# Graph kernel on one core: seven gathered slots in the third pass in place of six, counts scaled by ScalarE there

## The reference

```
for l in range(3):
    neigh = segment_sum(h[src], dst) / clip(deg, 1)
    h = h @ Ws_self[l] + neigh @ Ws_neigh[l] + bs[l]      (relu but for the last)
x = layernorm(x + h)
hs, hv = x[:, :128] @ w_in2f_s, einsum(x[:, 128:], w_in2f_v)     (32 + 3*32 numbers for each node)
W = (ssp(edge_attr_20 @ W1 + b1) @ W2 + b2) * edge_weight
edge = products of hs[idx_j], hv[idx_j], edge_attr_4 and W
agg = segment_sum(edge, idx_i)                            (idx_i = src, idx_j = dst)
x = layernorm(x + two small matrix products of agg)
```

## Time and profile before

| | us |
|---|---|
| median of 3 runs | 1892.74 (1888.39 to 1895.12) |
| profiled execution, its own time | 1891.2 |
| its span | 1889.4 |
| third pass, tile 50 to the last message row's store | about 1142 to 1457 |
| message phase | about 1459 to 1889 |
| busy PE, DVE, POOL, ACT | 1827.0, 1180.4, 1180.8, 627.3 |

### The profile page before, as it was taken

One profiled execution on the slowest core, in us unless ns is written; L12 is line 12 of the kernel. 1 busy time (PEld: TensorE's weight loads), 2 busy tenths in 40 slices (PEclk: granted clock), 3 DMA queues, 4 the chain that ended last, 5 costly groups with the idle time before them and its releaser, 6 DMA issues. The chain is left out here.

```text
span 1889.4 us, 23661 instructions
## 1 busy us (share of the span) xinstructions
PE 1827.0 (97%) x8259; PEld 1160.8 (61%) x8259; DVE 1180.4 (62%) x1811; ACT 627.3 (33%) x1432; POOL 1180.8 (62%) x1082
## 2 busy tenths in 40 slices
PE   7999999999999999999999998999998999999997
PEld 3454455555555555555555555666666888888886
DVE  5766678677644344343343344555553899999997
ACT  1566632233000000000000000111103888888885
POOL 4400000165588888888888883788886777777773
PEclk9999999999999999999999999999998999999999
DMA  5365566443454435444444434555564344434442
GB/s 156 108 218 182 202 217 185 124 115 104 129 143 138 123 107 147 134 134 124 117 130 122 114 98 156 179 190 195 195 196 133 89 116 116 113 108 107 108 117 56
DMA packets 235894, 261.88 MB, mean 139 GB/s; under 512 B 130678, under 2 KB 173280, under 8 KB 235773
## 3 DMA queue, kind: packets, MB, share of 16 engines
q1 hardware_dynamic: 200956, 204.29, 35.6%
q0 software_dynamic: 34032, 55.66, 11.0%
q10 hardware_dynamic: 784, 0.39, 0.1%
HBM read 172.52 MB, written 87.69 MB: 138 GB/s over the span
## 5 line engine op out<-in xcount | busy, mean ns | idle before, releaser
L1208 PE MATMUL low<-table,abuf 125*125 125x512 f16 x3750 | 835.2, 380 | 0.0
L1208 PEld LDWEIGHTS low<-table,abuf 125*125 125x125 bf16 x3750 | 506.4, 137 | 303.0 <-issue 27.9
L905 POOL DMA_INDIRECT by_src<-scat_row,sort x416 | 502.7, 1208 | 126.1 <-issue 118.8
L1037 PE MATMUL mid<-wbuf,h_t 128*125 128x512 f32 x1200 | 557.2, 601 | 14.0 <-DVE st_out L1733 10.9
L910 POOL DMA_INDIRECT table<-msg_table,wbuf x294 | 316.8, 1078 | 97.8 <-issue 97.5
L1037 PEld LDWEIGHTS mid<-wbuf,h_t 128*125 128x125 f32 x1200 | 214.9, 189 | 222.1 <-issue 198.2
L1743 DVE SCALAR_TENSOR_TENSOR y<-low,inv_deg,st_in 125x512 f32<-125x512 f32 x75 | 56.2, 749 | 446.6 <-PE low L1208 328.1
L1687 DVE TENSOR_TENSOR abuf<-abuf,row_scale 125x3125 bf16<-125x3125 bf16 (+4 forms) x87 | 256.9, 2956 | 1.2 <-DMA abuf<-adj 1.2
L937 POOL DMA_INDIRECT sort<-msg_table,sort x156 | 202.0, 1295 | 63.9 <-issue 47.2
L888 POOL TENSOR_TENSOR sort<-sort 128x416 f32<-128x416 f32 x26 | 31.8, 1224 | 329.9 <-DVE sort L1805 329.9
L1242 PE MATMUL low<-table,wbuf 128*125 128x256 f32 x900 | 209.9, 383 | 21.0 <-ACT table L1466 20.9
(11 more groups left out here) (244 smaller groups left out, 1616.6 us busy)
## 6 DMA issues: line engine op xcount, KB each, us to landing
abuf<-adj SPq DMA_DIRECT2D x75, 781.2 KB, 5.0
adj<-table SPq DMA_DIRECT2D x25, 781.2 KB, 4.5
states<-st_out SPq DMA_DIRECT2D x75, 256.0 KB, 2.3
st_in<-states SPq DMA_DIRECT2D x75, 256.0 KB, 4.9
flips<-y_flip SPq DMA_DIRECT2D x48, 256.0 KB, 4.3
h_t<-flips SPq DMA_DIRECT2D x192, 64.0 KB
early_rows<-sort POOLq DMA_DIRECT2D x30, 320.0 KB, 2.7
table<-early_rows SPq DMA_DIRECT2D x24, 384.0 KB, 6.5
```

The costliest lines, as they stand in the source:

```text
L905: pool.indirect_dma_start(out=by_src, out_offset=bass.IndirectOffsetOnAxis(ap=place_i[:, k * PIECE + j:k * PIECE + j + 1], axis=0), in_=sc ...
L1037: last = pe.matmul(to[0:TN, :], h_t[i % 2][:, k, 0:TN], weights[l % 2][:, a, k, :], start=k == 0, stop=k == KC - 1)
L1208: last = pe.matmul(p_agg[k % 2][0:TN, :], a_tile[k % 3][:, a, :], table[ps % 2][0:TN, a, h, :], start=a == 0 and h == 0, stop=a == TILES - ...
```

## The change

- Seven slots of every source tile (`EARLY = 7`) are gathered in the third pass, 35 steps in place of 30. The gathers, the store and the load of tile 0's second group go. In the message phase GpSimd gathers slots 7 to 17 of all 25 tiles: 275 gathers, 11 for each tile, tile 0 among them. The load of one tile's early slots is 448 KB where it was 384, and its buffer is waited for until group 1 (not 0) of two tiles back is through.
- For k = 52 to 74 the counts are scaled by ScalarE: 25 activations of 125x125 (L1403 of the changed file), 16 ahead of the eviction of the transposes and 9 behind it. TensorE waits for the two parts at `a = 0` and `a = 16`. VectorE's L1687 is left out for these tiles.

```diff
+EARLY = 7
+STEPS = EARLY * CHUNKS
@@
-            return 16 * (t // 2 + 1)
-        return 16 * GS * (t // 2 + (0 if g == 1 and t % 2 == 0 else 1))
+        return 16 * (t // 2 + 1) * {0: 1, 1: 2 * GS - EARLY}.get(g, GS)
@@
+        return {0: (0, 22, 23, 24, 25), 1: (0, 23, 25)}.get(k % TILES, (0, 16, 25) if k > 2 * TILES else (0, 25))
+
+    def by_act(k):
+
+        return 2 * TILES + 1 < k < AGGS
@@ load_early (SP)
-                    sp.wait_ge(s_gd, 3 * NG * (t - 2) + 3)
+                    sp.wait_ge(s_gd, 3 * (NG * (t - 2) + 1) + 3)
@@
-            sp.wait_ge(s_est[SECOND % 3], loads_of(SECOND, 3))
-            sp.dma_start(msg_slots[0][:, GS:2 * GS, :], second_rows.rearrange("p (j k) -> p j k", j=GS)).then_inc(s_second, 16)
@@ GpSimd, windows of the early slots
-            pool.dma_start(e_swin, edges_of[:, 0, GS:2 * GS, :]).then_inc(s_ewin[0], 16)
...
-                               edges_of[:, lo:hi, 0:GS, :].rearrange("p t j k -> p t (j k)")).then_inc(s_ewin[n], 16)
+                               edges_of[:, lo:hi, 0:EARLY, :].rearrange("p t j k -> p t (j k)")).then_inc(s_ewin[n], 16)
@@ GpSimd, early steps
-            steps_of = [(j, c) for j in range(GS) for c in range(CHUNKS)]
+            steps_of = [(j, c) for j in range(EARLY) for c in range(CHUNKS)]
...
-            gather_second()
             store_early(*steps_of[-1])
-            store_second()
@@ GpSimd, message phase
-                for g in range(1 if t else 2, NG):
+                for g in range(1, NG):
                     if t >= 2:
                         pool.wait_ge(s_gd, 3 * (NG * (t - 2) + g) + 3)
-                    for j in range(g * GS, (g + 1) * GS):
+                    for j in range(max(g * GS, EARLY), (g + 1) * GS):
@@ ScalarE
+            def scale(k, part):
+                parts = parts_of(k)
+                if part == 0:
+                    act.wait_ge(s_a[k % 3], loads_of(k, 3))
...
+                for a in range(parts[part], parts[part + 1]):
+                    last = act.activation(a_tile[k % 3][:, a, :], a_tile[k % 3][:, a, :], ACT.Copy, scale=row_scale[k // TILES % 2][0:TN, a:a + 1])
+                last.then_inc(s_as, 1)
@@
                     root(i - AGGS + 1)
+                    if by_act(k + 1):
+                        scale(k + 1, 0)
                     transposed(i, ACT.Copy)
+                    if by_act(k + 1):
+                        scale(k + 1, 1)
                     message_rows(i)
@@ VectorE
-                if k + 1 < AGGS:
+                if k + 1 < AGGS and not by_act(k + 1):
                     scale(k + 1, 0)
...
-                if t == 0 and g == 1:
-                    dve.wait_ge(s_second, 16)
-                else:
-                    dve.wait_ge(s_g[g][t % 2], slots_gathered(t, g))
+                dve.wait_ge(s_g[g][t % 2], slots_gathered(t, g))
```

More of the change, by code:

```diff
@@ L171, in gnn_kernel @@
     early = Region(sort_sb[:, :], 7 * CH * 4)
-    e_rows = [early.take(P, [GS, G]) for _ in range(3)]
-    e_idx = early.take(P, [TILES, GS], I32)
-    e_second = early.take(P, [GS], I32)
-    e_f = early.take(P, [GS, TILES])
-    e_fs = early.take(P, [GS])
-    e_max = early.take(P, [GS + 1])
-    e_most = early.take(1, [GS + 1])
-    e_below = early.take(1, [GS + 1, TILES])
-    e_need = early.take(1, [GS + 1], I32)
+    e_rows = [early.take(P, [FEW, G]) for _ in range(3)]
+    e_idx = early.take(P, [TILES, EARLY], I32)
+    e_f = early.take(P, [EARLY, TILES])
+    e_max = early.take(P, [EARLY])
+    e_most = early.take(1, [EARLY])
+    e_below = early.take(1, [EARLY, TILES])
+    e_need = early.take(1, [EARLY], I32)
     x_rows = Region(sort_sb[:, :], 7 * CH * 4).take(P, [SLOTS, G])
@@ L277, in gnn_kernel @@
     ereg = Region(wbuf[:, :, :].rearrange("p a k -> p (a k)"), 2 * 2 * KC * D * 4)
-    e_win = ereg.take(P, [TILES, GS, PAY])
-    e_swin = ereg.take(P, [GS, PAY])
+    e_win = ereg.take(P, [TILES, EARLY, PAY])
     treg = Region(tbuf[0][:, :], T_SIZE)
@@ L467, in early_gathered @@
     def early_gathered(s):
-        return 16 * sum(GS if n == SECOND else FEW for n in range(s % 3, s + 1, 3))
+        return 16 * FEW * (s // 3 + 1)
     def slots_gathered(t, g):
-        if g == 0:
-            return 16 * (t // 2 + 1)
-        return 16 * GS * (t // 2 + (0 if g == 1 and t % 2 == 0 else 1))
+        return 16 * (t // 2 + 1) * {0: 1, 1: 2 * GS - EARLY}.get(g, GS)
     def node_rows(t):
@@ L775, in _ @@
                 if k == AGGS - 4:
-                    sp.wait_ge(s_eidx, len(PARTS_OF) + 1)
+                    sp.wait_ge(s_eidx, len(PARTS_OF))
                 if k >= AGGS - 4 and k < AGGS - 1:
@@ L807, in load_early @@
                 if t >= 2:
-                    sp.wait_ge(s_gd, 3 * NG * (t - 2) + 3)
+                    sp.wait_ge(s_gd, 3 * (NG * (t - 2) + 1) + 3)
                 c, i = t // FEW, t % FEW
                 if t == 1 or i == 0:
-                    for j in range(GS):
+                    for j in range(EARLY):
                         s = early_step(j, c)
                         sp.wait_ge(s_est[s % 3], loads_of(s, 3))
-                sp.dma_start(msg_slots[t % 2][:, 0:GS, :], early_rows[:, c, :, i * G:(i + 1) * G].rearrange("j p k -> p j k")).then_inc(s_g[0][t % 2], 16)
+                sp.dma_start(msg_slots[t % 2][:, 0:EARLY, :], early_rows[:, c, :, i * G:(i + 1) * G].rearrange("j p k -> p j k")).then_inc(s_g[0][t % 2], 16)
             extras(sp, extra_round)
-            sp.wait_ge(s_est[SECOND % 3], loads_of(SECOND, 3))
-            sp.dma_start(msg_slots[0][:, GS:2 * GS, :], second_rows.rearrange("p (j k) -> p j k", j=GS)).then_inc(s_second, 16)
             for t in range(TILES):
@@ L915, in extra_round @@
                 wait_alone(pool, s_xl, q * 32)
-                for s in range(SECOND - 2, SECOND + 1):
+                for s in range(STEPS - 3, STEPS):
                     pool.wait_ge(s_est[s % 3], loads_of(s, 3))
@@ L1193, in _ @@
                         pe.wait_ge(s_emax, 1)
-                        for n in range(GS + 1):
+                        for n in range(EARLY):
                             top = pe.transpose(p_b[n // 4][0:1, n % 4 * P:(n % 4 + 1) * P], e_max[:, n:n + 1], ident[:, :])
@@ L1412, in bin_masks @@
                     act.activation(in_bins[k % 2], in_bins[k % 2], ACT.Relu, bias=1.0, scale=-1.0).then_inc(s_cols, 1)
+            def scale(k, part):
+                parts = parts_of(k)
+                if part == 0:
+                    act.wait_ge(s_a[k % 3], loads_of(k, 3))
+                if k == 2 * TILES + 2 and part == 0:
+                    act.wait_ge(s_row, AGGS)
+                    act.wait_ge(s_as, scaled_at[k, 0] - 1)
+                for a in range(parts[part], parts[part + 1]):
+                    last = act.activation(a_tile[k % 3][:, a, :], a_tile[k % 3][:, a, :], ACT.Copy, scale=row_scale[k // TILES % 2][0:TN, a:a + 1])
+                last.then_inc(s_as, 1)
             for k in range(AGGS):
@@ L1443, in _ @@
             act.wait_ge(s_acc, AGGS)
-            for j in range(GS):
+            for j in range(EARLY):
                 s = early_step(j, 0)
                 act.wait_ge(s_est[s % 3], loads_of(s, 3))
-            act.dma_start(msg_slots[0][:, 0:GS, :], early_rows[:, 0, :, 0:G].rearrange("j p k -> p j k")).then_inc(s_g[0][0], 16)
+            act.dma_start(msg_slots[0][:, 0:EARLY, :], early_rows[:, 0, :, 0:G].rearrange("j p k -> p j k")).then_inc(s_g[0][0], 16)
             def hots(t):
```

34 lines of the change are left out of this document (9 added, 25 removed).

## The result

| | before | after |
|---|---|---|
| median of 12 runs, us | 1891.43 (1888.14 to 1896.0) | 1894.92 (1892.1 to 1901.7) |
| profiled execution: its time, its span | 1891.2, 1889.4 | 1897.32, 1895.5 |
| VectorE's row of tile 49 to that of tile 74 (L1743, now L1737) | 325.10 | 324.88 |
| first instruction of (0,0) to that of (24,2) | 408.32 | 413.22 |

The ratio is 1.0026, with a 95% interval of 1.0014 to 1.0037, a loss of 2.6 to 7.0 us; the two medians stand 3.5 us apart. It is a loss clear of nothing, and as a ratio it is inside the 0.3% that the prediction called no change. The forecast was 4.9 us more than before. Its 1897.6 us started from a median of 1892.7 over three runs, where twelve runs give 1891.43. In what follows (t,g) is again a group of six slots, and "start of (t,g)" is VectorE's first instruction of it that needs the gathered rows (L1982 after, L1991 before).

A forecast was written before the change was run, and what follows sets the result against it. Steady message tiles were taken as bound by a loop of VectorE, ScalarE and TensorE, the third pass by TensorE. Terms 0.5 + 4.4 - 1.4 + 1.4 = +4.9 us on a median of 1892.7 gave 1897.6 us, range 1889 to 1903.

The forecast's parts named there:

- Scaling leaves VectorE: Third pass, 23 tiles: 3.41 us each leave VectorE, early gathers end about 24 us earlier; gain on the path nothing.
- ScalarE takes it over: Third pass: sixteen activations, 4.9 us, fit before the transposes end with 0.5 us to spare; cost nothing.
- Loads of indices: Tile 52's wait for the early slots' indices grows; cost 0.5 us, between 0 and 1.5.
- Start of the message phase: Tile 0 needs 11 gathers where it needed 6; VectorE is 4.4 us late from (1,2) on, bounds 3 and 6.
- the clock: TensorE pauses 2.3 and 3.1 us before the sums of (0,1), (0,2); its clock halves for 4 us: +1.4 us.
- landing: Time from a gather's start to the release of VectorE, taken as 4.0 us, with 3.6 as lower bound.
- The tiles behind: Message phase after the start: zero gain in 22 tiles, VectorE's three remaining waits for gathers go, 1.4 us less.
- B: Rival, start of the message phase: TensorE stays at 1.2 GHz for 10 us; +8.1 us, 1901; chance 0.22.
- D: Rival, steady tiles: GpSimd's gather stream paces them, so tiles fall to 16.3 us; sum -2.1, 1890.6; chance 0.13.
- E: Rival, message phase: each of 24 removed gathers frees VectorE for 0.95 us; sum -18, 1875; chance 0.06.
- F: Rival, third pass: GpSimd's stalls stay though VectorE no longer scales, early work ends late; +35, 1932; chance 0.03.
- C: Rival, third pass: ScalarE is late from 0.39 us an activation; at 0.5, +40 us, 1935; chance 0.07.

The follow-up runs named there:

- e2: Kernel before, with only the scaling of the counts in the third pass moved to ScalarE, six early slots kept; 1891.34 us, ratio 1.0001.
- e4b: The change, with TensorE making the filters of group (t,1) ahead of the next tile's hidden matmuls; 1895.31 us, ratio 1.0031 against the kernel before.
- e7: The change, with 3 and 18 unused short matmuls on TensorE ahead of the sums of (0,1) and (0,2); 1896.53 us, ratio 1.0035 against the kernel before.
- e1: The change's seven early slots alone, VectorE still scaling the counts; 1914.5 us, ratio 1.0132 against the kernel before.
- e3: The change, with slots 7 to 11 of tile 0 also gathered early in the third pass; 1890.63 us, ratio 0.9999 against the kernel before.
- e6b: e3 with TensorE's filters of (t,1) ahead of the next tile's hidden matmuls; 1888.86 us, ratio 0.9992 against the kernel before.
- e9: e6b with VectorE's one-hot rows of (t,2) made right behind (t,1), ahead of the hidden layer; 1887.85 us, ratio 0.9981 against the kernel before.
- e5b: Kernel before, with TensorE's filters of (t,1) ahead of the next tile's hidden matmuls, twelve gathers a tile; 1888.63 us, ratio 0.9991.
- e8: The change, with all 25 scaling activations ahead of the eviction of the transposes; ratio 1.0556, only in the job that can't be compared.

## Why the prediction was right, and where its terms were off

The sign, the size and the mechanism held: the change removes 30 us of gathers from an engine that nobody waits for, and pays for it once, at the start. By the terms of the sum:

- **Scaling leaves VectorE, 0 us on the path:** right. e2 gives 1.0001. The early gathers fell to a mean of 973 ns, and the last one starts at 1426.5, its store at 1433.3, where 1424 was forecast for the last store; the idle time ahead of the first message gather is 26.5 us in place of the 35 forecast. Nothing waits for either. The Trainium skill (SBUF — State Buffer, Who interferes with whom) doubts that tensor_tensor can stall the making of descriptors. For this instruction the traces speak against it: where VectorE scales, one gather in each tile takes 3.0 to 4.1 us, where ScalarE does, none is over 1.5.
- **ScalarE takes it over, 0 us:** right. 4.73 us for sixteen against 4.9 forecast, 0.80 us to spare against 0.5.
- **Loads of indices, +0.5:** not seen. From tile 49 to tile 52 the four kernels with seven columns take 54.1 to 56.8 us, the three with six 56.0 to 57.0. The term is 0 within the scatter of such stretches, 1.0 us with six columns and 2.6 with seven. TensorE's wait grew, 4.34 us against 3.18, but it was 1.69 in e4b: it takes up what earlier tiles left.
- **Start of the message phase, +4.4, and the clock, +1.4:** together 5.8 forecast, 6.1 measured: (1,2) is 33.62 us behind (0,0), where it was 27.50. Inside, the split was off. (0,2) is 6.2 late (6.0 forecast). The low clock costs 2.2 (e7) where 2.0 were forecast for (1,1), of which I let only 1.4 through to (1,2), taking that group to wait for its gather; it doesn't, gather 22 starts 5.5 us ahead of it. And "landing" was too long, 2.5 and 3.7 us behind the start of gathers 5 and 11 against 4.0, which the start-up stalls of the gathers made up: gather 11 starts 13.95 us behind gather 1, not 12.9. These errors cancel, so that 5.8 lies so near 6.1 is luck in part.
- **TensorE's pauses:** 0.76 and 4.54 us, where 2.3 and 3.1 were forecast. The clock fell 2.3 us into the second pause and was low from 1479.7 to 1486.5, 6.8 us. Only 4.5 of these fell on matmuls, where 4 were forecast.
- **The tiles behind, −1.4:** −1.2 measured (413.22 − 408.32 − 6.12). Zero in the steady tiles, as forecast.
- **Not in the sum:** the chain from the last row of the third pass to (0,0) took 10.82 us in the trace of after and 12.05 before. In after the last message product ran at full clock (1.08 us for eight matmuls, 1.89 in before). Over the nine profiled executions that can be compared (e1 aside, whose (0,0) waits for its early rows) it lies between 10.8 and 12.1, and kernels that are alike there have both values (10.85, 10.89 and 11.84 in e3, e6b and e9): a chance of one execution, worth as much as the clock term itself.

Sum by the traces, from the row of tile 49 to the start of (24,2): −0.2 + 6.1 − 1.2 − 1.2 = +3.5, and without the last term +4.7, beside 4.9 forecast.

Of the rivals, B is the nearest miss: the low stretch of 6.8 us is over the 6 that it named, but B counted every low microsecond on matmuls, and the 2.3 in the pause cost nothing; e7 prices the clock at 2.2 us, not 5.3. D fell with e5b. E (fewer gathers free VectorE) fell with the steady tile of 16.62 us with one gather less, and VectorE's L1982 is as long as L1991 was. F (the stalls stay) was what e1 does; priced at +35 it came to +25, for the six steps behind the last scaling (at 1422) take 6.9 to 7.6 us, not 8.9, and those with scalings beside them 8.7 on average. C did not occur; e8 shows that a late eviction is paid by TensorE, 0.96 us a tile for 25 activations ahead of it. (C's time for 0.5 us an activation should read 1937 by its own terms, not 1935.)

Where I was wrong was in what to expect of improvements: e3 was to gain 2 us and gained nothing measurable, and the tile of 16.3 us did not come with the filters first or with e9. I took the whole gap as a gain, as if VectorE's own row came next, and it is that short; but with the filters first the loop of TensorE and ScalarE takes 16.50 us. In the old order that loop is some 15.2 us, an estimate from the 1.3 us by which the hidden matmuls end earlier there.

## What to carry to other kernels

Work taken from an engine with slack is worth nothing however large it is, but where that engine's first results are awaited, one instruction more is paid in full; price a change of "how much ahead" at the start of the phase first, tile 0 above all, and then the steady state. If a change takes work from one tile's preparation to give to all, keep the first tile's: e3 is free of the change's loss. And before a gap is counted as a gain, look for the loop that comes next: follow each engine that waits once in a tile back to what released it, and add up that round, one without the engine with the gap among them. Moving a step out of one loop may put it into another, as the hidden matmuls here. A gap of 0.12 us that the profile names no one for can still be a wait.

## What the runs showed of the hardware that was not expected

- One VectorE instruction of 3.4 us (bf16 tensor_tensor, 125x3125) makes one indirect DMA on GpSimd take 3.0 to 4.1 us in place of 0.95, 21 times each in before and e1. The other way there is little: the first instruction of a group (L1982 and its like) takes 743 to 774 ns in before and after, with 275 to 294 gathers beside it, and at most 830 over the ten traces that can be compared; the eleven that pass 775 all have a gather that starts within 0.04 us of them.
- A gather releases VectorE between 2.5 and 4.0 us after its start (5 and 11 of the change, 11 of e7), less for an early one of the row than for one amid a full stream. Why is open.
- After TensorE had issued nothing for 2.3 us at 1477.4 to 1479.7, the granted clock fell from 1.00 to 0.50, its 1.2 GHz level, and it stayed there for 4.5 us of matmuls; with short matmuls in the pause (e7) it stayed at 1.00, though 0.82 us of idle time was left.
- VectorE's neighbours with no wait between them start 0.08 us before the one ahead has ended (L1991 to L1994 in before, L1986 behind L2026 in e9); one that needs the result ahead of it starts 0.03 us behind its end (L2000 to L2004 in before).
- One chip slowed these programs by 1% to 5.6% against a kernel before that was itself 110 us slower there, by stops of TensorE inside runs of matmuls and of ScalarE ahead of an eviction. The kernels with ScalarE's 25 activations a tile lost some 150 us in the third pass from tile 52 on, the one without 5.6, all of it at its end. So a placement that costs nothing on one chip may cost on another; what the stops are isn't known.
